# Cross attention: the sixteen context projections of a token tile spread over four quarters, the half-batches taken in another order, two rotary-key buffers

## What is computed

```python
def xattn(hidden_q, kv_c, Wq, w_kc_q, w_kc_kv, W_qr, W_kr, Wo):    # 16 heads, context rows of 128
    q_big = einsum('bshk,hkq->bshq', (hidden_q @ Wq.T).reshape(b, s, H, K), w_kc_q)
    kv_rope = kv_c * cos[None] + _rotate_half(kv_c) * sin[None]
    scores = einsum('bhsr,bhlr->bhsl', einsum('bshq,hqr->bhsr', q_big, W_qr),
                    einsum('bld,hdr->bhlr', kv_rope, W_kr))
    ctx_c = einsum('bhsl,bld->bhsd', softmax(scores), kv_rope)
    return einsum('bhsd,hkd->bshk', ctx_c, w_kc_kv).reshape(b, s, H * K) @ Wo.T
x = x + xattn(layernorm(x), ctx_512, ...)
x = x + self_attention(layernorm(x), ...)
x = x + mixture_of_experts(layernorm(x), ...)
```

## Time and profile before

| what | value |
|---|---|
| time, median of 3 runs | 1540.34 us (1539.63 to 1545.67) |
| the profiled execution | 1537.91 us, of which its span (first to last instruction) 1536.1 us |
| cross stage | from 154.66 us (first transpose) to 801 us |
| one tile of the cross stage | four quarters, here 242.58 to 320.55 us: 77.97 us |
| mean granted TensorE clock | 0.952 |

### The profile page before, as it was taken

One profiled execution on the slowest core, in us unless ns is written; L12 is line 12 of the kernel. 1 busy time (PEld: TensorE's weight loads), 2 busy tenths in 40 slices (PEclk: granted clock), 3 DMA queues, 4 the chain that ended last, 5 costly groups with the idle time before them and its releaser, 6 DMA issues. The chain is left out here.

```text
span 1536.1 us, 22738 instructions
## 1 busy us (share of the span) xinstructions
PE 1358.9 (88%) x7136; PEld 1104.9 (72%) x7136; DVE 800.6 (52%) x1362; ACT 735.7 (48%) x1741; POOL 575.1 (37%) x346
## 2 busy tenths in 40 slices
PE   5997799999999999999966999997799989999950
PEld 4775577777777777777744888886677767887740
DVE  4433465757575656565624444443499832333225
ACT  2443465656565655555524677777411223333320
POOL 2122232333333333333013333332356494259826
PEclk9999799999999999999987999998899999999985
DMA  5796540504141313232415111113643266456537
GB/s 201 236 288 176 214 163 1 201 19 177 41 167 51 139 79 128 91 123 96 178 43 183 45 63 56 48 48 103 235 151 110 90 233 213 151 179 246 179 99 216
DMA packets 78984, 209.79 MB, mean 137 GB/s; under 512 B 5888, under 2 KB 39168, under 8 KB 72960
## 3 DMA queue, kind: packets, MB, share of 16 engines
q1 hardware_dynamic: 69472, 163.78, 30.1%
q0 software_dynamic: 7136, 38.80, 7.4%
q10 hardware_dynamic: 2304, 6.29, 1.1%
HBM read 154.59 MB, written 92.01 MB: 161 GB/s over the span
## 5 line engine op out<-in xcount | busy, mean ns | idle before, releaser
L660 DVE TENSOR_TENSOR probsT_lo<-psTr,probsT_hi 128x512 fp32r<-128x512 f32 x256 | 176.4, 690 | 200.5 <-ACT probsT_hi L610 200.2
L610 ACT CAST probsT_hi<-psTr 128x512 fp32r<-128x512 f32 x256 | 150.0, 586 | 211.7 <-PE psTr L750 210.9
L750 PE MATMUL psTr<-ident,probs 128*128 128x128 f32 x1024 | 152.6, 276 | 18.9 <-DVE probsT_lo L660 12.9
L750 PEld LDWEIGHTS psTr<-ident,probs 128*128 128x128 f32 x1024 | 122.2, 141 | 62.3 <-DVE probsT_lo L660 29.1
L527 POOL TENSOR_TENSOR ctxT_lo<-ctx_f,ctxT_hi 128x512 fp32r<-128x512 f32 x32 | 41.3, 1292 | 321.1 <-ACT ctxT_hi L579 321.1
L655 DVE TENSOR_REDUCE nmax<-psS 128x1 f32<-128x1024 f32 x128 | 155.4, 1214 | 11.5 <-PE psS L66 10.7
L572 ACT ACTIVATE probs<-psS,nmax 128x1024 f32<-128x1024 f32 x128 | 143.5, 1121 | 28.5 <-DVE nmax L655 28.5
L64 PE MATMUL bank<-w_slots,ao_first_hi 128*128 (+1 forms) x252 | 107.0, 425 | 16.1 <-DVE w_slots L1731 9.3
L64 PE MATMUL psV<-probsT_hi,kv_hi 128*128 128x512 f32 x256 | 117.3, 458 | 2.0
L64 PE MATMUL psS<-kT_hi,qe 128*128 128x512 f32 x256 | 112.9, 441 | 5.6 <-issue 4.7
L1461 POOL TENSOR_TENSOR w_slots<-w_ahead,w_slots 128x3072 fp32r<-128x3072 f32 x15 | 102.2, 6811 | 1.2
(11 more groups left out here) (258 smaller groups left out, 3321.4 us busy)
## 6 DMA issues: line engine op xcount, KB each, us to landing
w_ahead<-w_exp POOLq DMA_DIRECT2D x14, 1536.0 KB, 7.3
qe<-stage SPq DMA_DIRECT2D x16, 1024.0 KB, 6.7
qe<-qe SPq DMA_DIRECT2D x16, 1024.0 KB, 5.1
wraw<-w_pairs SPq DMA_DIRECT2D x8, 1792.0 KB, 11.3
early<-xs SPq DMA_DIRECT2D x47, 256.0 KB, 3.0
xs<-h_rows SPq DMA_DIRECT2D x47, 256.0 KB, 2.0
early<-ctx SPq DMA_DIRECT2D x16, 512.0 KB, 3.5
ao<-attn_out SPq DMA_DIRECT2D x32, 256.0 KB, 2.4
```

What stands on the lines that cost most here:

```text
L610: act.copy(PT[k % PTN].hi[:], psT[slot][:]).then_inc(turned_hi, 1)
L660: dve.tensor_tensor(out, psT[slot][:], f32(hi), ALU.subtract).then_inc(turned_free, 1)
L750: last = pe.transpose(psT[slot][:, q * P:(q + 1) * P], src(q), ident[:])
```

## The change

The order of half-batches becomes sequence 0 heads 0 to 7, sequence 1 heads 0 to 7, sequence 0 heads 8 to 15, sequence 1 heads 8 to 15. So heads 0 to 7 of a tile can be projected from its own quarter 2 on. The table `HEADS_AT` says after which step a head stands: quarter 2 and 3 project heads 0 to 7 of their own tile, quarter 0 and 1 of the next tile heads 8 to 15. Both keys of a tile must be at hand in turn now: the K turns stand in quarters 2 and 3 for the next tile, in steps 2 and 5 (before: quarters 0 and 2, steps 2 and 6), and the rotary keys have a buffer each (`kv_rope` of two, the new one is `kv_rope_second`). For room, `probsT` has 3 buffers in place of 4 (`PTN`). The rotary keys of sequences 0 and 1 are made in the query stage, after its 2nd and 4th weight pair; the second context load stands there too. The steps of the norm move to quarter 1 step 7 up to quarter 2 step 4.

```diff
@@ build_queries, SP
-        with sp.Fori(0, NP // 2 - 1) as i:
+        for p in range(2):
+            step(p, p, True)
+        sp.wait_ge(keep["rope_done"], 2)
+        sp.dma_start(keep["kv_raw"], t["ctx"][1]).then_inc(keep["kv_in"], 16)
+        with sp.Fori(1, NP // 2 - 1) as i:
@@ build_queries, POOL
-        with pool.Fori(0, NP // 2) as i:
+        pool.sem_inc(keep["rope_done"], 1)
+        for i in range(2):
             for j in range(2):
                 split_low(j, 2 * i + j)
-        pool.sem_inc(keep["rope_done"], 1)
-        pool.wait_ge(keep["tab_in"], 16)
-        rope_kv(pool, keep, 0)
+            if i == 0:
+                pool.wait_ge(keep["tab_in"], 16)
+            rope_kv(pool, keep, i, i)
@@ tables
-PTN = 4
-K_STEPS, R_STEP = (2, 6), 4
+PTN = 3
+K_STEPS, R_STEP = (2, 5), 4
+HEADS_AT = {0: {1: (8,), 3: (9,), 5: (10,), 7: (11,)}, 1: {0: (12,), 2: (13,), 4: (14,), 6: (15,)},
+            2: {5: (0,), 6: (1,), 7: (2,)}, 3: {0: (3,), 2: (4,), 4: (5,), 6: (6,), 7: (7,)}}
...
-        if hf == 0 and has_k and k in K_STEPS:
+        if c >= 2 and has_k and k in K_STEPS:
@@ POOL, per quarter
+                if c == 2 and not first:
+                    root(i - 1)
                 if not (first and c == 0):
                     ctx_low(n - 1, (c - 1) % HB)
...
+                if c == 0:
+                    kv_low(2 * i + 1, 1)
+                if c == 3 and not last:
+                    kv_low(2 * i + 2, 0)
+                if c < 2 and not last:
...
+                    rope_kv(pool, keep, 2 * i + 2 + c, c)
@@ ScalarE, per step
-                    act.wait_ge(pv_done, LT * n + k + 1)
+                    wait(act, pv_done, LT * n + k - PTN + 1 if k >= PTN else LT * n - LT + (LT - 2, LT - 1, LT - 3)[k] + 1)
...
-                    if k == 3 and hf == 0 and has_k:
-                        kv_high(b + 1, 1 - j)
+                    if k == 3 and c == 0:
+                        kv_high(2 * i + 1, 1)
+                    if k == 3 and c == 3 and not last:
+                        kv_high(2 * i + 2, 0)
@@ VectorE
-        LN_STEPS = {1: residual, 3: stats, 4: aggregate, 5: variance}
+        LN_STEPS = {(1, 7): residual, (2, 0): stats, (2, 1): aggregate, (2, 2): variance, (2, 3): norm}
...
-                        if (c, k) == (2, 7):
+                        if (c, k) == (2, 4):
                             h2_low(i - 1)
@@ PE
                 if h == 0:
                     pe.wait_ge(h2_lo, tt + 1)
-                    pe.wait_ge(ct_lo, HB * tt + HB)
+                    pe.wait_ge(ct_lo, HB * tt + 3)
                 if h == H // 2:
-                    pe.wait_ge(ct_lo, HB * tt + HB + 1)
+                    pe.wait_ge(ct_lo, HB * tt + 5)
...
-                    if not first:
-                        if c == 0:
-                            project(i - 1, range(2 * k, 2 * k + 2))
-                        if (c, k) == (2, 5):
-                            turn_h2(i - 1)
-                    if last and c == 3 and k >= 2:
-                        project(i, range(max(0, k - 2) + min(k - 2, 2), k - 1 + min(k - 1, 2)))
+                    if not first and (c, k) == (2, 4):
+                        turn_h2(i - 1)
+                    if c >= 2 or not first:
+                        project(i if c >= 2 else i - 1, HEADS_AT[c].get(k, ()))
```

More of the change, by code:

```diff
@@ L470, in build_cross, with place, halves, tiles @@
     AT = {True: turn_counts(True), False: turn_counts(False)}
[L472 to L482, removed]
+    def place(i, c, what, k, has_k):
+        g, m = AT[has_k][(c, what, k)]
+        return FIRST + TURNS * i + g + 1, FIRST + SPLITS * i + m + 1, FIRST + SPLITS * i + m + 1 + 2
+    def halves(i, c, last):
+        return HB * i + c, c % 2, c // 2, not last, not (last and c == HB - 1)
+    def tiles(eng, iteration):
+        iteration(0, True, False)
+        with eng.Fori(1, NT - 1) as i:
+            iteration(i, False, False)
+        iteration(NT - 1, False, True)
     block = ctx.enter_context(nc.Block())
@@ L487, in _, with load_kv, load_qe, fill @@
     def _(sp):
[L488 to L491, removed]
+        for done in keep["cleared"]:
+            sp.sem_clear(done)
+        def load_kv(b):
+            sp.wait_ge(rope_done, b + 1)
+            sp.dma_start(kv, kv_d[b]).then_inc(kv_in, 16)
+        def load_qe(b, j):
+            sp.dma_start(QE[j][:].bitcast(F32), qe_d[b]).then_inc(qe_in[j], 16)
+        def fill(r):
+            sp.dma_start(t["xs_r"][r], t["zeros"]).then_inc(keep["fill_in"], 16)
+        for j in range(2):
+            load_qe(j, j)
+        sp.dma_start(XT[:], x_d[0]).then_inc(xt_in, 16)
+        def iteration(i, first, last):
+            if not last:
+                fill(2 * i)
+                for j in range(2):
+                    load_kv(2 * i + 2 + j)
             if not first:
[L493 to L496, removed]
                 sp.wait_ge(x1_made, i + 1)
                 sp.dma_start(XT[:], x_d[i]).then_inc(xt_in, 16)
[L500 to L508, removed]
+            if not last:
+                for j in range(2):
+                    sp.wait_ge(s_mm, RT * (HB * i + 3 + j))
+                    load_qe(2 * i + 2 + j, j)
+                fill(2 * i + 1)
+        tiles(sp, iteration)
+        for r in range(2 * NT - 2, NBLK // NT):
+            fill(r)
         sp.wait_ge(rope_done, B + 1)
         sp.dma_start(keep["early"][0], t["w_qkv"][0]).then_inc(keep["wqkv_in"][0], 16)
-        sp.wait_ge(turned, place(B - 2, 0, "K", 1, True)[0])
-        sp.wait_ge(kv_lo, B)
+        sp.wait_ge(turned, place(NT - 2, 2, "K", 1, True)[0])
+        sp.wait_ge(kv_lo, B - 1)
         sp.dma_start(keep["early"][1], t["w_qkv"][1]).then_inc(keep["wqkv_in"][1], 16)
@@ L534, in _ @@
         kv_low(0, 0)
-        pool.wait_ge(turned, 2)
-        pool.wait_ge(kv_lo, 1)
-        rope_kv(pool, keep, 1)
         def iteration(i, first, last):
             for c in range(HB):
-                n, b, j, hf, has_k, more = half_steps(i, c, first, last)
+                n, j, hf, has_k, more = halves(i, c, last)
+                if c == 2 and not first:
+                    root(i - 1)
                 if not (first and c == 0):
                     ctx_low(n - 1, (c - 1) % HB)
[L544 to L556, removed]
+                if c == 0:
[3 more added lines that the diff above has]
+                if c < 2 and not last:
+                    if first:
+                        pool.wait_ge(turned, 2 * c + 2)
+                    else:
+                        pool.wait_ge(turned, place(i - 1, 2 + c, "K", 1, True)[0])
+                    pool.wait_ge(kv_lo, 2 * i + c + 1)
+                    rope_kv(pool, keep, 2 * i + 2 + c, c)
+        tiles(pool, iteration)
         ctx_low(HB * NT - 1, HB - 1)
@@ L831, in _ @@
+        tiles(pe, iteration)
         project(NT - 1, range(H // 2, H))
```

180 lines of the change are left out of this document (91 added, 89 removed).

## The result

The changed kernel takes 1565.46 us (median of 4 runs, 1563.82 to 1567.23) against 1541.01 us of the kernel before in the same comparison: ratio 1.0153, with a 95% interval of 1.0129 to 1.0178. The change makes the kernel 24 us slower. Forecast were 1567 us, range 1549 to 1578.

What follows compares the result with a forecast made beforehand. The prediction took PE to bound the cross stage, with only its waits able to shrink or grow. Its terms summed to +29.4 us on the profiled 1537.9, giving a forecast of 1567 us, range 1549 to 1578.

Steps and rivals of the forecast that it cites:

- wait of head 8: Quarter 0, step 1, tiles 1 to 7: PE waits 2.85 us each for `ctxT_lo`, +20.0 us.
- clock behind it: Behind head 8's gap: granted clock falls to half in four of seven tiles, 1.7 us each, +6.8 us.
- quarter 1: Heads 11 to 14 ahead of turn P of step 5 cover its 0.64 us wait, -4.5 us.
- quarter 3: New K turns there: waits at turns P of steps 3, 4 and 6, 1.31 in place of 0.64 us, +4.7 us.
- quarter 2: Its 0.80 and 0.66 us waits stay; the moved norm adds 0.1 us a tile at head 0, +0.7 us.
- start and tile 0: Two more K turns hide in the gap before the first scores; turns and waits leave tile 0, -1.0 us.
- query stage: Added context load beside busy DMA engines costs between 0 and 1.9 us; taken as +1.5 us.
- The most that the idea can give: All PE waits in the cross stage that filling could remove: 2.74 us per tile, 22 us over 8 tiles.
- The faster rival: Heads fill the gaps and `ctxT_lo` is there in time at head 8: 1519 us, chance 0.08.
- The rival of a half wait: Head 8 waits 1.4 us, clock holds, quarter 3 loses nothing more: 1546 us, no change, chance 0.12.
- the two cases of the clock: Behind head 8: clock holds, 1560 us, chance 0.15; or falls each time, 1577 us, chance 0.08.
- the rival at 1577: Clock falls behind head 8 each time, +11.9 us, and quarter 3 loses its upper bound, +9; chance 0.08.

Runs made afterwards that it cites:

- experiment 1: Changed kernel with heads 8 to 10 of quarter 0 after steps 3, 4, 5 instead of 1, 3, 5: 1535.83 us, ratio 0.9979 to the kernel before.
- experiment 2: Changed kernel with eight extra matmuls, result overwritten, on PE ahead of head 8's wait: 1555.98 us, ratio 1.0122 to the kernel before.
- experiment 7: Kernel before with three buffers of `probsT` in place of four, nothing else: 1540.59 us, ratio 1.0002.
- experiment 5: experiment 1 with `ctxT_hi` made in step 0 of every quarter: 1531.50 us, ratio 0.9947 to the kernel before.
- experiment 6: experiment 5 with `kT_lo` of the first K turn ahead of the row maximum, second K turn in step 6, head 0 after step 6: 1520.41 us.
- experiment 8: Kernel before with `ctxT_hi` made in step 0 of every quarter, nothing else: 1534.70 us, ratio 0.9954.
- experiment 4: Changed kernel with the second K turn back in step 6 instead of 5: 1566.70 us, ratio 1.0193 to the kernel before.
- experiment 3: Changed kernel with `ctxT_hi` made in step 0 instead of 1, in quarter 0 alone: 1546.59 us, ratio 1.0064 to the kernel before.
- experiment 10: experiment 6 with both rotary keys made behind all eight weight pairs, second context load behind the seventh: 1524.80 us, ratio 0.9898 to the kernel before.
- experiment 9: experiment 8 with `kT_lo` of the first K turn ahead of the row maximum: 1533.39 us, ratio 0.9946 to the kernel before.

## Why the prediction was right, point by point

The cross stage from the first scores matmul to the last `ctx_f` took 625.7 us before and 651.6 after: 25.9 us of the 27.8 of the span. Ahead of it the changed kernel took 1.1 us less (first scores at 160.23 and 161.34), behind it 3.0 us more. That last stretch varies by 5 us among the profiles, and the 3.0 include the half clock behind the gap at the end of the last tile (last section).

| term of the sum | forecast, us | what the runs show |
|---|---|---|
| wait of head 8 | +20.0 | 7 x 2.77 = +19.4, gone in experiment 1 |
| clock behind it | +6.8 | 7 of 7 tiles at half clock, 1.52 each: +10.6 (experiment 2) |
| quarter 1 | -4.5 | 18.86 us with 3 heads more than before (2.08) against 17.59: 7 x -0.81 = -5.7 |
| quarter 3 | +4.7 | both waits there, 0.67 and 0.51; net of K turns and heads 7 x 0.45 = +3.2 |
| quarter 2 | +0.7 | 19.68 against 18.22 with two heads more (1.38): 7 x 0.08 = +0.6 |
| quarter 2, last tile | +1.2 | 18.46 us against 16.51, with two heads more: +0.6 |
| start and tile 0 | -1.0 | first scores to first `ctx_f` 29.98 against 31.49: -1.5 |
| query stage | +1.5 | not seen, open |
| three buffers | 0 | 0 in the old order (experiment 7) |

The measured terms but the last two add up to +27.2 us. Quarter 3 of the last tile, for which the forecast had no term, took 14.27 us against 16.42 with two heads fewer (1.38): -0.8. That makes 26.4, and 25.9 were measured.

*What bounds the kernel.* The reading that PE bounds the cross stage, and that only its waits can shrink or grow, held. PE's 7136 matmuls were the same in all kernels but that of experiment 2, and the changes of the cross stage could be read as waits at turns or heads and the clock behind them.

*The most that the idea can give* was put at 2.74 us a tile. The fastest kernel of the series is 77.97 - 75.68 = 2.29 us a tile below the kernel before, within that bound, and needed two edits beside the new order.

*The mechanism* that decided was the one forecast: one head placed ahead of data that PE's own turn has to set in motion. The faster rival failed as argued, since the wait of 2.77 us alone is larger than all that could be gained. The rival of a half wait failed. Of the two cases of the clock all seven falls came true, though without the upper bound of quarter 3 that the rival at 1577 had with it. Taking four of seven was the step that was mis-sized in number, and 1.7 us a time was too high against the measured 1.5, so the term was 3.8 us short. That quarter 1 gained more, that quarter 3 lost less than forecast and that the query stage cost nothing that can be seen made up for it.

*Luck.* That the time lies only 1.5 us from the forecast is in part luck. These errors of terms cancelled, and so did two others: the forecast added 29.4 us to the profiled 1537.9, while the medians differ by 24.5 (1541.01 and 1565.46; the profiled executions, 1537.91 and 1565.76, by 27.9). A step 4.9 us too large stood on a base 3.1 us too low.

*A slip* stands in what was to show it: the quarters were said to take about 20.5, 18.5, 19.5 and 19.5 us, which is 78.0 and not the 81 to 83 of the tile in the same sentence. The prediction's own prices and waits, with ten heads and a pair of K turns out of quarter 0 and three, two and five heads more between the marks of quarters 1, 2 and 3, give 22.0, 19.0, 19.7 and 21.2; measured are 22.5, 18.9, 19.7 and 21.0. The sum went by waits and did not use the four figures. The rival with only quarter 1 gained comes to 1533.9, not 1533.

Not tried: the norm's place on VectorE was not moved by itself, so the 1.46 us of waits in the first half of quarter 2, where `psX` is taken and no head can stand, have been reduced only by the edits of experiments 5 and 6. The traces before and after show one thing that bears on it: the norm (`h_tile`) takes 1.46 to 1.53 us in the seven tiles in which GpSimd runs `ctxT_lo` at the same time, and 0.55 us in the last tile, where GpSimd runs nothing beside it. In experiment 8, where `ctxT_lo` starts earlier, it takes about 0.8 us in most tiles. Quarter 2 gained no more by that edit than quarters 1 and 3, which have no norm (0.24 or 0.25 us each); what a place away from `ctxT_lo` would give by itself is not measured.

## What to carry to other kernels

When work is spread to fill gaps on the bound engine, ask of the first item in each group when its operand is ready, counted from the engine's own instruction that sets the chain in motion; here moving it two steps on turned a loss of 24 us into a gain of 3. A wait in the middle of an engine that is otherwise full costs its length and, if it is long enough, the half clock behind it, so a gap of 2.5 us of idle time on PE is priced here at 4.3: 2.77 us late and 1.5 for the clock. Compare the sum of all waits that filling can remove with the one that it may add before touching the order.

## What the runs showed of the hardware that was not expected

The granted clock fell behind each of the seven gaps with 2.53 us of idle time in the changed kernel, and behind each of the seven in experiment 4, and behind none of the gaps of 0.70 us (experiment 2) or 0.80 us (experiment 3). Before, the clock held behind the gap of 2.14 us and fell behind one of 2.56, whose end on the time line of PE is

```profile
173.57 0.99 PE L750 MATMUL psTr<-ident,probs 128*128 128x128 f32 x4 [2.56 <-ACT probs L572]
```

The gap at the end of the last tile is as long in the changed kernel as before (2.13 us), and this time the clock fell behind it. The windows up to it and behind it:

```profile
811.80:814.60 2.80, 0.67 (x4) 0.23 (x2) 0.69 (x1) 0.62 (x1) 1.26 (x1) 1.00 0.08 32
814.70:818.10 3.40, 3.40 (x9) 2.63 (x10) 0.00 (x0) 0.00 (x0) 0.00 (x0) 0.50 0.01 2
```

This gap is 2.13 to 2.15 us in all twelve profiles; the clock fell behind it in seven (the changed kernel and experiments 4, 5, 6, 7, 8 and 10) and held in five (before and experiments 1, 2, 3 and 9). So a gap near 2.1 us can go either way, also between kernels whose instructions around it are the same, and one of 2.5 us should be counted as a fall. The Trainium skill, "TensorE: Matmul & The Clock Gate", section "What's actually happening", says that the throttled state is the default and activity lifts it; experiment 2 agrees, where extra matmuls in the gap kept the clock at 1.00 and bought 10.6 us.
